# First FFN of a two-layer decoder on one Trainium2 core: the ternary down product in float32r on two pieces, with its calls in a written-out order

## What is computed

```python
xq = activation_quant(rms_norm(x))
g = jax.nn.silu(ternary_matmul(xq, W_g))
u = ternary_matmul(xq, W_u)
p = g * u
return ternary_matmul(p, W_d)
# ternary_matmul(x, w) = jnp.matmul(x, jnp.sign(w).T); W_g, W_u: 1024 x 256; W_d: 256 x 1024
```

## Time and profile before

| | us |
|---|---|
| median of three runs | 770.2 |
| the three runs | 772.96, 769.62, 770.2 |
| span of the profiled execution, from the first to the last instruction | 767.8 |
| TensorE busy in it (matmul) | 714.2 |
| VectorE busy | 624.8 |
| GpSimd busy | 539.5 |
| ScalarE busy | 409.4 |
| mean granted TensorE clock (share of full speed) | 0.992 |

### The profile page before, as it was taken

One profiled execution on the slowest core, in us unless ns is written; L12 is line 12 of the kernel. 1 busy time (PEld: TensorE's weight loads), 2 busy tenths in 40 slices (PEclk: granted clock), 3 DMA queues, 4 the chain that ended last, 5 costly groups with the idle time before them and its releaser, 6 DMA issues. The chain is left out here.

```text
span 767.8 us, 13506 instructions
## 1 busy us (share of the span) xinstructions
PE 714.2 (93%) x4302; PEld 495.1 (64%) x4302; DVE 624.8 (81%) x1281; ACT 409.4 (53%) x656; POOL 539.5 (70%) x781
## 2 busy tenths in 40 slices
PE   5999999999997899999889999989899999999994
PEld 5777777654443577778667777765444457777783
DVE  4778877689797877775798999977999998787774
ACT  1666666620443444445487778870100348877885
POOL 2767889877667343341347877799887988999962
PEclk9999999999999999999999999999999999999998
DMA  8800000000400050000032111104000000000001
GB/s 285 362 30 2 2 2 3 1 1 1 164 0 1 0 209 2 1 1 1 5 110 83 55 56 56 55 1 126 1 1 1 0 2 1 9 22 15 15 22 35
DMA packets 12724, 33.37 MB, mean 43 GB/s; under 512 B 2672, under 2 KB 8048, under 8 KB 11376
## 3 DMA queue, kind: packets, MB, share of 16 engines
q1 hardware_dynamic: 12656, 32.52, 11.7%
HBM read 30.35 MB, written 2.16 MB: 42 GB/s over the span
## 5 line engine op out<-in xcount | busy, mean ns | idle before, releaser
L1170 PE MATMUL bank<-XT,win_late 128*128 128x256 f32 x320 | 84.1, 391 | 4.7 <-DVE ss_xc L1420 4.1
L684 DVE TENSOR_REDUCE MIX<-m_pr 128x128 f32<-128x1024 f32 x64 | 77.4, 1210 | 0.8
L1420 DVE SCALAR_TENSOR_TENSOR ss_xc<-bank,cw_late,ss_xc 128x254 f32<-128x254 f32 x144 | 66.8, 477 | 5.3 <-ACT ss_xc L1293 1.7
L632 POOL TENSOR_TENSOR m_kv<-XT,CTXT 128x512 f32<-128x512 f32 x64 | 67.7, 1082 | 4.1 <-PE bank L657 4.1
L632 POOL TENSOR_TENSOR m_kv<-CTXT 128x512 f32<-128x512 f32 x64 | 64.8, 1039 | 7.5 <-PE bank L657 7.5
L655 PE MATMUL bank<-m_kv,toep 128*128 128x512 f32 x128 | 67.4, 609 | 0.8 <-POOL m_kv L632 0.7
L541 POOL TENSOR_TENSOR f_ve<-f_mv,eps 128x1 f32<-128x1 f32 x48 | 9.7, 202 | 81.9 <-DVE f_mv L972 57.7
L1170 PEld LDWEIGHTS bank<-XT,win_late 128*128 128x128 f32 x320 | 55.9, 190 | 16.7 <-DVE ss_xc L1420 9.7
L656 PE MATMUL bank<-m_kv,toep 128*128 128x512 f32 x128 | 65.7, 595 | 0.0
L657 PE MATMUL bank<-m_kv,toep 128*128 128x512 f32 x128 | 65.4, 592 | 0.0
L1761 PE MATMUL bank<-had_last,f_ht 128*128 128x256 f32 x256 | 60.6, 383 | 2.9 <-ACT f_ht L1844 1.6
(11 more groups left out here) (245 smaller groups left out, 1890.5 us busy)
## 6 DMA issues: line engine op xcount, KB each, us to landing
MIX<-cum_rows SPq DMA_DIRECT2D x15, 512.0 KB, 3.6
toep<-toep_dram SPq DMA_DIRECT2D x2, 2048.0 KB, 11.7
X<-x_dram SPq DMA_DIRECT2D x1, 2048.0 KB, 12.6
CTXT<-ctxT_dram SPq DMA_DIRECT2D x1, 2048.0 KB, 17.6
out_dram<-f_o SPq DMA_DIRECT2D x16, 128.0 KB, 1.7
XT<-xT_dram SPq DMA_DIRECT2D x1, 1280.0 KB, 8.3
win_late<-win_dram SPq DMA_DIRECT2D x1, 1280.0 KB, 5.4
wgu<-wgu_dram SPq DMA_DIRECT2D x1, 1024.0 KB, 5.0
```

Source lines behind the costliest of these rows:

```text
L632: m = nc.gpsimd.tensor_tensor(KV[n % 3][:, c, :, :].rearrange("p (b j) i -> p b j i", b=HB), ki, vj, ALU.mult)
L684: nc.vector.tensor_reduce(head(MIX)[:, :, a, bass.ts(h, HB), :], PR[n % 2][:, :, :, :].rearrange("p c (b j) i -> p c b j i", b=HB), op=ALU ...
L1170: m = nc.tensor.matmul(bX[(NU * g + n) % 3][:, 0:GS_], win[:, h, off:off + P], XT[:, h, bass.ts(g, GS_)], start=(h == 0), stop=(h == C - 1))
L1420: m = nc.vector.scalar_tensor_tensor(acc[:, :, sh:S], bank[:, :, 0:S - sh], cw[:, r, n:n + 1], acc[:, :, sh:S], ALU.mult, ALU.add)
```

## The change

The down product no longer runs as a float32 product of p. p is split into two float32r pieces: `high` is a copy of p by ScalarE into a tile of type float32r (which rounds it), `low` is p minus `high`, by GpSimd. `down(n,0)` multiplies all eight pieces of `high`, `down(n,1)` all eight of `low`, and both add up in the same bank. The sign matrix becomes a float32r tile of its own, made by ScalarE at the end of its mixer list instead of in place in the middle. The buffers PMT, PH and PL are two each. The new tiles lie in space of the state space's tiles that are not yet in use (`brief`). All engine lists of f0 are now written out as a whole (`whole_run`), the mixer's last steps in them too, in another order; more calls of the last items stand in the state space's `begin`, and `a_exp` has moved there from the head of ScalarE's list to just ahead of `dt_exp`. Some waits on an engine's own earlier results are new.

The core of the diff (the lists cut to some lines each):

```diff
-        nc.scalar.activation(T["wd0"][:, :, :], T["wd0"][:, :, :], ACT.Sign).then_inc(s["signed"], 1)
...
+        act.wait_ge(s["signed"], 5)
+        nc.scalar.activation(T["wd0_signs"][:, :, :], T["wd0"][:, :, :], ACT.Sign).then_inc(s["signed"], 1)
...
-            pe.wait_ge(s[f"p{k}_kept"], n + 1)
+            part, pieces = (("high_made", PH), ("low_made", PL))[k]
+            pe.wait_ge(s[part], n + 1)
             if k == 0:
                 upto(pe, s["down_free"], n)
                 if n == 0:
                     pe.wait_ge(mixed["multed"], 60)
-            for r in range(4 * k, 4 * k + 4):
-                m = nc.tensor.matmul(b6[:, 0:D], PMT[n % 2][:, r, :], wd[:, r, :], start=(r == 0), stop=(r == FC - 1))
+                    pe.wait_ge(mixed["signed"], 6)
+            for r in range(FC):
+                m = nc.tensor.matmul(b6[:, 0:D], pieces[n % 2][:, r, :], wd[:, r, :], start=(k == 0 and r == 0), stop=(k == 1 and r == FC - 1))
...
+        def whole_run(mix):
+            mix(26); mix_turn(0); mix(27); mix_turn(1); mix(28); mix(29); mix_turn(2); mix(30); mix(31); q_turn(0); q_turn(1); mix_turn(3); gate(0, 1)
+            up(0, 1); gate(0, 0); up(0, 0); mix_turn(4); gate(1, 1); up(1, 1); p_turn(0, 1); p_turn(0, 0); gate(1, 0); mix_turn(5); up(1, 0)
...
+            gate(8, 0); up(8, 0); mix_turn(11); q_turn(9); down(6, 0); x_turn(2); gate(9, 1); p_turn(8, 1); down(6, 1); p_turn(8, 0); up(9, 1)
+            mix_turn(12); up(9, 0); gate(9, 0); q_turn(10); down(7, 0); down(7, 1); p_turn(9, 1); gate(10, 1); x_turn(3); up(10, 1); p_turn(9, 0)
...
+            upto(act, s["low_made"], n - 1)
+            nc.scalar.copy(PMT[n % 2][:, 4 * k:4 * k + 4, :], bP[k][:, :].rearrange("p (r s) -> p r s", r=4)).then_inc(s[f"p{k}_kept"], 1)
+
+        def high(n):
+            if not 0 <= n < B:
+                return
+            for k in range(2):
+                act.wait_ge(s[f"p{k}_kept"], n + 1)
             upto(act, s["downed"], n - 1)
-            nc.scalar.copy(PMT[n % 2][:, 4 * k:4 * k + 4, :], bP[k][:, :].rearrange("p (r s) -> p r s", r=4)).then_inc(s[f"p{k}_kept"], 1)
+            nc.scalar.copy(PH[n % 2][:, :, :], PMT[n % 2][:, :, :]).then_inc(s["high_made"], 1)
...
+        def whole_run():
+            keep_q(0); keep_q(1); silu(0, 1); silu(0, 0); silu(1, 1); keep_p(0, 1); keep_p(0, 0); high(0); silu(1, 0); keep_q(2); keep_p(1, 1)
...
+            high(4); keep_p(5, 1); silu(6, 1); keep_p(5, 0); high(5); silu(6, 0); keep_q(7); keep_p(6, 1); silu(7, 1); keep_x(0); keep_p(6, 0)
...
+            upto(dve, s["normed"], n - 1)
+            upto(dve, s["normed3"], n - 1)
...
+        def whole_run(times_q, add_up):
+            add_up(25); times_q(26); add_x(0); add_up(26); add_x(1); stats(0); stats(1); times_q(27); times_q(28); aggregate(0); aggregate(1)
+            add_up(27); add_up(28); norm_x(0); norm_x(1); peak(0); peak(1); times_q(29); add_x(2); step_size(0); step_size(1); stats(2); lift(0)
+            lift(1); quantise(0); quantise(1); add_up(29); aggregate(2); times_q(30); times_q(31); add_x(3); multiply(0, 1); stats(3); norm_x(2)
...
+            lift(9); stats(10); quantise(9); stats3(5); aggregate(10); add_x(11); multiply(8, 1); multiply(8, 0); stats(11); norm_x(10); peak(10)
+            norm_out(4); step_size(10); add_down(6); lift(10); quantise(10); add_x(12); stats3(6); aggregate(11); multiply(9, 1); norm_out(5)
+            multiply(9, 0); norm_x(11); peak(11); stats(12); step_size(11); add_down(7); stats3(7); aggregate(12); lift(11); quantise(11)
...
+        def low(n):
+            if not 0 <= n < B:
+                return
+            pool.wait_ge(s["high_made"], n + 1)
+            upto(pool, s["downed"], n - 1)
+            nc.gpsimd.tensor_tensor(PL[n % 2][:, :, :], PMT[n % 2][:, :, :], PH[n % 2][:, :, :].bitcast(F32), ALU.subtract).then_inc(s["low_made"], 1)
+
+        def whole_run(mix):
+            mix(26); mix(27); mix(28); mix(29); mix(30); rstd(0); rstd(1); mix(31); rms(0); step_back(0); rms(1); step_back(1); rstd(2); rstd(3); rms(2)
+            rms(3); low(0); rstd(4); step_back(2); step_back(3); rms(4); low(1); rstd(5); rms(5); rstd3(0); step_back(4); low(2); rstd(6); step_back(5)
+            rstd3(1); rms(6); low(3); rstd(7); step_back(6); rstd3(2); low(4); rms(7); rstd(8); step_back(7); rms(8); low(5); rstd3(3); rstd(9)
+            step_back(8); low(6); rms(9); step_back(9); rstd(10); rstd3(4); rms(10); low(7); rstd3(5); rstd(11); rms(11); step_back(10); low(8)
+            rstd3(6); rstd3(7); rstd(12); step_back(11); low(9); rms(12); step_back(12); rstd(13); low(10); rstd3(8); rstd(14); rms(13); rms(14)
+            step_back(13); step_back(14); low(11); rstd3(9); rstd(15); low(12); rstd3(10); rms(15); step_back(15); rstd3(11); low(13); low(14)
+            rstd3(12); rstd3(13); low(15); rstd3(14); rstd3(15)
...
+        def begin(f0_gate, f0_up, f0_p_turn, f0_down, f0_x_turn):
+            unit(0, 0); f0_down(13, 0); f0_down(13, 1); f0_p_turn(15, 1); f0_p_turn(15, 0); f0_down(14, 0); f0_x_turn(9); f0_down(14, 1); unit(0, 1)
...
+            tap3(0, 0); f0_keep_p(15, 1); f0_keep_p(15, 0); f0_high(15); f0_keep_x(9); tap3(0, 1); f0_keep_x(10); tap3(0, 2); f0_keep_x(11)
+            f0_keep_x(12); f0_keep_x(13); f0_keep_x(14); tap3(0, 3); f0_keep_x(15); tap3(0, 4); tap3(0, 5); a_exp(); dt_exp(); gate(0, 0); gate(0, 1)
```

More of the change, by code:

```diff
@@ L20 @@
 BF16 = mybir.dt.bfloat16
+F32R = mybir.dt.float32r
 ALU = mybir.AluOpType
@@ L68, in sb, with brief @@
         return self.scope.enter_context(self.nc.sbuf_tensor(name, shape, dt, side=self.side))
+    def brief(self, name, count, shape, dt):
+        with ExitStack() as own:
+            return [own.enter_context(self.nc.sbuf_tensor(f"{name}{k}", shape, dt, side=self.side)) for k in range(count)]
     def bank(self, name):
@@ L726, in ffn0 @@
     SL, PM, Y2 = two("sl", [P, FF]), two("pm", [P, FF]), two("y2", [P, D])
-    PMT = two("pmt", [P, FC, S])
+    PMT, PH, PL = two("pmt", [P, FC, S]), T["down_high"], T["down_low"]
     ST, MV, VE, RS = two("st", [P, 6]), two("mv", [P, 2]), two("ve", [P, 1]), two("rs", [P, 1])
@@ L734, in ffn0 @@
     bG, bU, bP = [b0, b1], [b2, b3], [b4, b0]
[L735 removed]
+    X, XT, MIX, ident, identb, wgu, wd = (T[n] for n in ("X", "XT", "MIX", "ident", "identb", "wgu0", "wd0_signs"))
     def sync(sp):
@@ L833, in x_turn @@
             m.then_inc(s["x_turned"], 1)
[L835 to L851, removed]
@@ L855, in scalar @@
+        return whole_run, gate, up, p_turn, down, x_turn
     def scalar(act):
@@ L1003, in gpsimd @@
+        return whole_run, multiply, add_down, stats3, norm_out
     def gpsimd(pool):
@@ L1033, in step_back @@
             nc.gpsimd.tensor_tensor(INV[n % 4][:, :], MS[n % 4][:, :], RS2[n % 2][:, :], ALU.mult).then_inc(s["inv_made"], 1)
-        def step(i):
-            rstd(i)
-            rms(i)
-            rstd3(i - 3)
-            step_back(i)
-        def begin(mix):
-            mix(26); rstd(0); rstd(1); rms(0); mix(27); mix(28); mix(29); mix(30); rms(1); step_back(0); mix(31); step_back(1); rstd(2); rms(2)
-            rstd(3); step_back(2); rstd(4); rms(3); rms(4); rstd3(0); step_back(3); rstd(5); rstd3(1); step_back(4); rstd3(2); rms(5); step_back(5)
-        return step, begin
+        def low(n):
[12 more added lines that the diff above has]
+            rstd3(12); rstd3(13); low(15); rstd3(14); rstd3(15)
+        return whole_run, low, rstd3
     return Stage(sync, tensor, scalar, vector, gpsimd)
@@ L1105, in state_space @@
     ROW, LA = [spare[:, k] for k in range(2)], [spare[:, 2 + k] for k in range(2)]
-    XC, SZ = two("xc", [P, CC, GS_]), two("sz", [P, 4, GS_])
+    XC = two("xc", [P, CC, GS_])
+    T["wd0_signs"] = ch.brief("f0_wd", 1, [P, FC, D], F32R)[0]
+    SZ = two("sz", [P, 4, GS_])
+    low1 = ch.brief("f0_plb", 1, [P, FC, S], F32R)
     XS = two("xs", [P, DI])
-    Y1, Y2, SQ, CBM = two("ysum", [P, 4, S]), two("y2", [P, 4, S]), two("sq", [P, 4, S]), two("cbm", [P, S])
+    T["down_high"] = ch.brief("f0_ph", 2, [P, FC, S], F32R)
+    Y1, Y2 = two("ysum", [P, 4, S]), two("y2", [P, 4, S])
+    T["down_low"] = ch.brief("f0_pla", 1, [P, FC, S], F32R) + low1
+    SQ, CBM = two("sq", [P, 4, S]), two("cbm", [P, S])
     VY, RY = two("vy", [P, 1]), two("ry", [P, 1])
@@ L2215, in _ @@
                     run(mix, n_mixed, n_last)
-                    step, begin, *f0_last = f0.tensor(pe)
-                    begin(mix)
-                    run(step, n_first, nf)
+                    whole, *f0_last = f0.tensor(pe)
+                    whole(mix)
                     (step, begin, end), mix = st.tensor(pe), m1.tensor(pe)
@@ L2230, in _ @@
                     m0.scalar(act)
-                    step, begin, *f0_last = f0.scalar(act)
-                    begin()
-                    run(step, n_first - 3, B)
+                    whole, *f0_last = f0.scalar(act)
+                    whole()
                     step, begin, end = st.scalar(act)
@@ L2246, in _ @@
```

(10 more changed lines are left out.)

106 lines of the change are left out of this document (54 added, 52 removed).

## The result

The changed kernel takes **762.37 us** (median of 4 runs, 762.06 to 765.02) beside 771.24 us of the kernel before on the same chip: a ratio of 0.9894 [0.9869, 0.9919], 8.9 us or 1.1% faster. The profiled execution spans 760.4 us in place of 767.8, which is 7.4 less: a run's time lies some 2.0 us above its span (762.45 above 760.4), so the profiled execution of the kernel before was one of its faster ones. The direction was right and the time lies inside the range, but the forecast was 19 us of gain: more than half did not come.

The account below looks back on a forecast made before the run. TensorE was taken to bound f0, VectorE after the change; steps 13, start 4 and end 2 make 19 us off the 767.8 us span, 748.8, plus 2.4 for the median: 751.2 us, range 742 to 767.

Parts of the forecast that it names:

- The bound: In f0 the step passes from TensorE (6.77 us before, 5.0 after) to VectorE, whose list needs 5.27.
- the 5.27: VectorE's list per step of f0: 6.77 us less two waits of 0.61 and 0.89.
- Four per step would pay 1.1: VectorE's delay by low in f0: 0.28 us for each of four instructions, half taken, 0.55, for a step of 5.8.
- The 0.66: Mean excess in us of a VectorE normalisation in the state space, where GpSimd is busy for 38.98 of 50 us.
- The upper end, 1.57 for each low: Upper end of the f0 step, 6.84 us: each low holds up one VectorE instruction for 1.57 us.
- The low's price: GpSimd's subtraction of 1024 elements in f0 takes 1.93 us, so its list needs 5.12.
- float32r: On TensorE in f0's down product, each of 16 float32r calls per item takes 0.109 us.
- The start: At the start of f0 the new order takes back 4 us of TensorE's waits; ends 0 and 7.
- The end: From the last products of f0 to the last kept x: -2 us, ends -3.5 and +3.
- The rival of the two engines that drag each other: In f0 VectorE and GpSimd delay each other: a step of 6.4 us, 760 us in all; chance 0.18.
- The pace rival: float32r keeps float32's pace, 0.216 us per call, TensorE's step stays 6.77: 769 us; chance 0.10.
- that of two instructions: float32r runs as two instructions per call, 54 us more on TensorE in f0: some 823 us; chance 0.05.

Follow-up runs that it names:

- e8: The change with TensorE making only one of the eight calls on the low piece, which is still made in whole; 763.00 us.
- e1: The change with low computed for only one column of each 128 from item 2 on; 745.67 us.
- e6: The change with lift moved from VectorE to ScalarE, low left whole; 761.26 us.
- e11: The change with norm_x, norm_out and quantise written as scalar_tensor_tensor and lift moved to ScalarE; 765.37 us.
- e12: The change with low subtracting the first 128 columns of high, read eight times as a broadcast, in place of the whole piece; 764.39 us.
- e3: The change's new order alone, with the float32 down product of the kernel before and neither high nor low; 766.11 us.
- e2: The change with the one-column low from item 2 on, and four one-column powers on GpSimd ahead of it as filling; 750.38 us.
- e10: The change with VectorE's norm_x, norm_out, lift and quantise written as scalar_tensor_tensor, low whole; 770.75 us.

## Why the prediction was right in part

- **The bound.** Right for the change: VectorE's own list sets the step. It is busy for 81.4 of 85 us, and its normalisations wait for no other engine (0.0 in their row). TensorE is off the bound (e8). That the step of 5.22 without the low (e1) comes near the 5.27 taken from two waits in one step of the earlier trace rows is luck: in the middle of e1 a step is 4.80, and TensorE is as full there as VectorE. So VectorE's list was taken some 0.5 us too long, which hid a part of the next error.
- **The step that failed** is this: "Four per step would pay 1.1, but only the first to meet a low waits, so I take half, 0.55". The 0.66 behind it was an average of the state space, scaled by how long GpSimd is busy, as if VectorE met a low by chance. It was then halved, as if a low that one instruction misses were lost. In f0 VectorE has almost no gaps, and four of its instructions per step can be caught; so nearly each low catches one (in the change's trace just one of them is lengthened, by more than 0.1 us, under 14 of the 16 lows, and none under the other two). The standing is about half the low: 1.29 against 2.38 / 2 = 1.19, as it would be if a low were met at any point of its length alike, which is argued and not shown. e6 and e11 show that the low catches what comes: remove one victim and the next stands. Of the 1.29, 1.22 reach a step in the middle of f0, and 0.93 the average of the 15 (e1). The upper end, 1.57 for each low, was the better side of that bound.
- **The low's price.** 2.38 us, not 1.93. The row was "of the same form" by name and size, but one of its inputs is a broadcast column; the trace of before has two inputs without a broadcast too, in its last stage. What makes the row shorter is open (e12).
- **float32r.** 0.120 to 0.130 us per call, not 0.109, in one instruction; TensorE paused for 15.5 of 85 us in the change, so it cost nothing there.
- **The start** was right in size, 4.0 us, and in part by luck. The mixer's last product starts 7.2 us earlier (244.87, before 252.12): the waits of 3.75 and 0.66 us are gone, another of 0.66 too, and from 235 to 240 us the granted clock was 0.76 before and is 1.00 now. But TensorE now waits at the first turns and gates of f0, 3.3 us in four waits, of which these are the longest:

```profile
246.95 0.28 PE L776 MATMUL bank<-identb,f_q 128*128 128x128 bf16 x2 [1.06 <-DVE f_q L969]
...
249.84 0.81 PE L781 MATMUL bank<-wgu,f_qt 128*128 128x512 bf16 x3 [1.56 <-DVE m_pr L680]
```

- **The end** had the wrong sign: +1.6 in place of -2, since the new order leaves three items' sums behind the last product (e3, 16.4 us), and the normalisations there meet lows: 2.32 and 1.86 us at 343.90 and 350.43. Without the lows the end is 12.0 (e1).
- **What the sum left out**: 3.5 us behind f0. The wait of the dt copy behind nine taps, which I could have read in the order, costs 1.3 to 1.6 in every kernel with that order, e3 included; 1.7 goes with the lower clock around the end of the state space.
- **The rival of the two engines that drag each other** (760 us) was the nearest number. Its mechanism is only a small part: VectorE's normalisations do not wait for GpSimd in the change, and e2 gives GpSimd's longer list 0.15 us per step. The pace rival and that of two instructions fell.

Together: -4.0 - 8.5 + 1.6 + 3.5 = -7.4 us of span, where -19 was forecast. Of the 11.6 us that did not come, 4.5 lie in the steps, 3.6 in the end of f0 and 3.5 behind it.

## What to carry to other kernels

When wide work is put on GpSimd beside a VectorE that is the bound, expect each such instruction to hold up one VectorE instruction that works from SBUF to SBUF, whichever comes. Here that was 1.04 to 1.29 us for one of 2.38 us (seven kernels), 0.32 to 0.44 for a half of 1.30, and 0.08 for a quarter of 0.74. Look for the cost inside VectorE's durations (mean against minimum), since no idle time shows it. Cut the wide instruction in two and move work off VectorE together: the change is 1.1% faster than the kernel before, either step alone brings that to 1.4%, which is not clear of the noise, and both bring it to 2.2%. And compare executions at the same granted clock before a difference of a few us is explained.

## What the runs showed of the hardware that was not expected

- The standing is handed on: 287 ns of quantise became 853 when lift left VectorE (e6).
- A wide GpSimd subtraction of two plain inputs takes 0.74, 1.30 and 2.38 us for 256, 512 and 1024 elements, and neither float32r output nor a block broadcast changes it.
- It works both ways: in e10 GpSimd's one-column additions (L547) take 0.33 to 0.38 us where they fall into a lift or quantise of the two-input form, and 0.19 elsewhere; their mean rose from 207 to 243 ns.
- The same pause of TensorE can leave its granted clock alone or not. At the start of f0 TensorE was busy for 1.83 of the 5 us from 245 to 250 in the change and for 1.85 in e3; in the next 5 us the clock was 1.00 in the change and 0.50 in e3.
